# An S4D + dense + LoRA tower on one core: the first two x1 tiles turned by TensorE in fp32, four W2 squares and the bias pass moved

## The reference

```python
# tok: the S4D kernel, L = 1024 steps
dt  = exp(log_dt);  A = -exp(inv_A_real) + 1j*A_imag;  dtA = A*dt[:, None]
Cc  = B[None]*x_complex * (exp(dtA) - 1) / A
h   = 2 * real(einsum('chn,hnl->chl', Cc, exp(dtA[:, :, None]*arange(1024))))
# attn: layernorm without gain, then a dense 1024 x 1024 product
h   = h + (layernorm(h) @ attn_W.T + attn_b)
# ffn: layernorm, dense product, and a mixture of 4 LoRA experts of rank 8
z   = layernorm(h)
h   = h + (z @ W.T + b) + sum_e softmax(z @ Wr.T)_e * 2 * ((z @ A_e.T) @ Bm_e.T)
```

## Time and profile before

| what | value |
|---|---|
| time, median of 3 runs | 831.0 us (828.77 to 832.25) |
| the profiled execution's own time | 829.42 us |
| its span | 827.6 us |
| mean granted clock of TensorE | 0.987 of full |
| TensorE busy | 792.3 us, 96% |
| VectorE busy | 583.2 us, 70% |
| ScalarE busy | 394.8 us, 48% |
| DMA moved | 70.17 MB |

### The profile page before, as it was taken

How to read it: one execution, slowest core, us unless ns; L and a number is a source line. 1 busy time by engine, 2 the same in 40 slices (tenths; PEclk the granted TensorE clock), 3 DMA queues, 4 the chain that set the end, 5 groups by cost and what they waited for, 6 DMA issues and landing times.

```text
span 827.6 us, 15856 instructions
## 1 busy us (share of the span) xinstructions
PE 792.3 (96%) x5974; PEld 410.0 (50%) x5974; DVE 583.2 (70%) x1136; ACT 394.8 (48%) x778; POOL 7.1 (1%) x20
## 2 busy tenths in 40 slices
PE   3678899999999999999999999999999999999998
PEld 3653445554554455455545554555455545554543
DVE  7889786766757777776768777676877767676533
ACT  4658643626454462636355272645436264642210
POOL 2000000000000000000000000000000000000000
PEclk9889999999999999999999999999999999999999
DMA  7637633424332232334232333433324243323323
GB/s 273 192 72 160 121 77 71 92 54 95 76 79 67 64 82 65 81 76 93 62 80 57 76 78 67 95 76 63 70 64 95 52 94 76 89 51 76 53 51 76
DMA packets 185563, 70.17 MB, mean 85 GB/s; under 512 B 174080, under 2 KB 179072, under 8 KB 185544
## 3 DMA queue, kind: packets, MB, share of 16 engines
q1 hardware_dynamic: 185448, 69.80, 36.9%
q10 hardware_dynamic: 96, 0.13, 0.0%
HBM read 11.96 MB, written 16.78 MB: 35 GB/s over the span
## 4 chain that ended last, share of the span: by engine, by line
PE 89%; DVE 7%; ACT 2%; issue 1%; DMA 0%; SPq 0%; DVEq 0%; ACTq 0%
PE ps_g L523 38%; PE ps_g L463 38%; PE ps_a L455 7%; PE ps_g L534 2%; PE ps_g L651 1%; PE ps_p L511 1%; DVE wa_lo L1181 1%; DVE params L932 1%; DVE m_im L1042 1%; PE ps_p L513 1%; DVE h_tok L1051 0%; DVE m L1042 0%; PE ps_p L528 0%; ACT phase L690 0%; DVE y L1076 0%
## 5 line engine op out<-in xcount | busy, mean ns | idle before, releaser
L463 PE MATMUL ps_g<-wa_hi,x 128*128 128x512 f16 x1024 | 271.5, 381 | 2.9 <-DMA x<-x_tok 2.2
L523 PE MATMUL ps_g<-wf_hi,x 128*128 128x512 f16 x992 | 265.2, 380 | 1.7 <-DVE h_tok L1090 1.7
L463 PEld LDWEIGHTS ps_g<-wa_hi,x 128*128 128x128 f16 x1024 | 97.9, 98 | 123.2 <-issue 7.4
L463 PE MATMUL ps_g<-wa_lo,x 128*128 128x512 f16 x512 | 154.0, 380 | 0.0
L523 PE MATMUL ps_g<-wf_lo,x 128*128 128x512 f16 x496 | 149.2, 380 | 0.0
L523 PEld LDWEIGHTS ps_g<-wf_hi,x 128*128 128x128 f16 x992 | 95.0, 98 | 107.8 <-issue 2.5
L716 ACT ACTIVATE junk<-ps_a,stat 128x1024 bf16<-128x1024 f32 x32 | 35.7, 1114 | 121.8 <-DVE stat L1054 121.8
L736 ACT ACTIVATE x_tok<-y 128x1024 f16<-128x1024 f32 x32 | 33.8, 1057 | 125.3 <-DVE y L1076 125.3
L1152 DVE SCALAR_TENSOR_TENSOR result<-ps_g,unscale,h_tok 128x1024 f32<-128x1024 f32 x31 | 39.8, 1284 | 72.1 <-PE ps_g L534 72.1
L463 PEld LDWEIGHTS ps_g<-wa_lo,x 128*128 128x128 f16 x512 | 50.3, 98 | 60.6 <-issue 1.0
L722 ACT ACTIVATE junk<-h_tok,stat 128x1024 bf16<-128x1024 f32 x32 | 36.7, 1147 | 91.1 <-DVE stat L1094 91.1
(11 more groups left out here) (188 smaller groups left out, 759.5 us busy)
## 6 DMA issues: line engine op xcount, KB each, us to landing
out<-result SPq DMA_DIRECT2D x124, 128.0 KB, 2.2
stage<-in_L_ffn_W SPq DMA_DIRECT2D x8, 512.0 KB, 8.5
x_raw<-in_x SPq DMA_DIRECT2D x38, 64.0 KB
h_tok<-in_L_attn_weight SPq DMA_DIRECT2D x2, 512.0 KB, 4.1
x<-in_L_attn_weight SPq DMA_DIRECT2D x2, 512.0 KB, 7.6
result<-in_L_attn_weight SPq DMA_DIRECT2D x2, 512.0 KB, 9.2
x<-x_tok SPq DMA_TRANSPOSE x64, 3.2
x<-stage SPq DMA_TRANSPOSE x64, 2.8
```

What stands on the lines that cost most here:

```text
L463: mm = pe.matmul(ps[:, o, :], x1_part(part, ps is ps_g2)[:, k, :], ws[:, k, o * HALF:(o + 1) * HALF], start=k == 0 and part == 0 and ws is ...
L523: pe.matmul(ps_g2[:, o, :], xs[:, k, :], ws[:, k, o * HALF:(o + 1) * HALF], start=k == 0 and xs is x2_hi and ws is wf_hi, stop=False)
```

## The change

- x1 of the sub-tiles (0, 0) and (0, 1) is no longer split to `x1_tok` and turned by DMA. TensorE turns `y` in fp32, in two halves of four transposes, into `ps_x` and `ps_p` (`turn_first_x1`). ScalarE copies each half to the high part of x1 (`high_first`), VectorE subtracts it from PSUM for the low part (`low_first`). The counts of `s_x1`, `s_hi1`, `s_lo1` are two sub-tiles lower from then on (`X1_BY_PE`).
- In TensorE's order the squares of the W2 blocks 8 to 11 stand ahead of the q transposes. Before, 8 and 9 stood behind `turn_weight(0)`, and 10 and 11 behind `s4(0, 0)`.
- The second pass over the bias on ScalarE moves from behind `first_decays(1)` to ahead of the copies of q, and the small op on VectorE that it needs to the front of its order.
- `weight_norms(1)` moves ahead of `normalise_1(0, 0)` and writes its product to a free part of `params`.
- The orders of `ffn_hi`/`ffn_lo` for blocks 8 and 9, of `attn_hi`/`attn_lo` and of `make_m(0, 1)` shift around these; `SPLITS` and `LOWS` follow.

```diff
-SPLITS = (0, 1, 2, 3, 4, 5, 8, 6, 9, 7, 10, 11, 12, 13, 14, 15)
-LOWS = (0, 1, 2, 3, 4, 5, 8, 6, 7, 9, 10, 11, 12, 13, 14, 15)
+SPLITS = (0, 1, 2, 3, 4, 5, 6, 8, 7, 9, 10, 11, 12, 13, 14, 15)
+LOWS = (0, 1, 2, 3, 4, 5, 6, 7, 8, 9, 10, 11, 12, 13, 14, 15)
+X1_BY_PE = 2
...
@@ sync
             sp.wait_ge(s_norm, 2)
-            turn_x1(0, 0)
             load_x(1)
             turn_weights(KB, KB + 1)
             sp.wait_ge(s_wt, KB)
             load_lora_a(wg_rows, s_wg)
-            turn_x1(0, 1)
             turn_weights(KB + 1, KB + 5)
@@ tensor
+            def turn_first_x1(i):
+                pe.wait_ge(s_xn1, i + 1)
+                for half, ps in enumerate((ps_x, ps_p)):
+                    for k in range(4):
+                        block = 4 * half + k
+                        mm = pe.transpose(ps[:, k * P:(k + 1) * P], y[:, block * P:(block + 1) * P], ident[:, :])
+                    mm.then_inc(s_yt, 1)
...
             turn_x(0)
+            pe.wait_ge(s_pre_act, 3)
+            square_ffn(KB, KB + 4)
             pe.wait_ge(s_pre_act, 6)
...
             turn_weight(0)
-            pe.wait_ge(s_xt_sb, 1)
-            pe.wait_ge(s_pre_act, 3)
-            square_ffn(KB, KB + 2)
             pe.wait_ge(s_top, 1)
             turn_weight(1)
             pe.wait_ge(s_q, 2)
             s4(0, 0)
-            square_ffn(KB + 2, 2 * KB)
+            square_ffn(KB + 4, 2 * KB)
             square_lora_a()
...
             turn_weight(3)
+            pe.wait_ge(s_xt_sb, 1)
+            pe.wait_ge(s_top, 2)
+            turn_first_x1(0)
             pe.wait_ge(s_wlo, low_done(3))
             turn_weight(4)
-            pe.wait_ge(s_top, 2)
+            pe.wait_ge(s_lo1_half, 2)
             turn_weight(5)
+            attn_part(0, 0, range(0, 4), (0,))
             pe.wait_ge(s_wlo, low_done(4))
             turn_weight(6)
-            pe.wait_ge(s_x1, 32)
-            attn_part(0, 0, range(0, 4), (0,))
             s4(0, 1)
...
-            attn_part(0, 0, range(KB), (1,)).then_inc(s_g1, 1)
+            attn_part(0, 0, range(0, 5), (1,))
+            turn_first_x1(1)
+            attn_part(0, 0, range(5, KB), (1,)).then_inc(s_g1, 1)
+            pe.wait_ge(s_lo1_half, 4)
             turn_x(1)
             turn_lora_a()
-            pe.wait_ge(s_x1, 64)
             attn_part(0, 1, range(0, 6), ps=ps_g2)
@@ scalar
+            def high_first(i):
+                for half, ps in enumerate((ps_x, ps_p)):
+                    act.wait_ge(s_yt, 2 * i + half + 1)
+                    act.activation(x1_part(0, i == 1)[:, 4 * half:4 * half + 4, :],
+                                       ps[:, :].rearrange("p (k o) -> p k o", o=P), ACT.Copy).then_inc(s_hi1_half, 1)
...
-            high_1(0, 0)
-            attn_hi(2, 3)
-            attn_hi(4, 5)
+            attn_hi(2)
+            high_first(0)
+            attn_hi(3, 4, 5)
+            attn_hi(6)
             ffn_hi(8)
-            attn_hi(6)
-            ffn_hi(9)
             attn_hi(7)
             square_1(0, 1)
             rstd_guess(0, 1, stat_1, s_ssq1, s_log1, s_y1)
+            ffn_hi(9)
+            high_first(1)
             ffn_hi(10)
-            high_1(0, 1)
@@ vector
+            def low_first(i):
+                for half, ps in enumerate((ps_x, ps_p)):
+                    part = slice(4 * half, 4 * half + 4)
+                    dve.wait_ge(s_hi1_half, 2 * i + half + 1)
+                    dve.tensor_tensor(x1_part(1, i == 1)[:, part, :], ps[:, :].rearrange("p (k o) -> p k o", o=P),
+                                      x1_part(0, i == 1)[:, part, :], ALU.subtract).then_inc(s_lo1_half, 1)
...
             keep_h(0, 0)
             attn_lo(0, 1)
+            weight_norms(1, ps_p[:, 0:P])
             normalise_1(0, 0)
-            low_1(0, 0)
-            attn_lo(2, 3)
-            dve.wait_ge(s_lo1, 1)
-            weight_norms(1, ps_p[:, 0:P])
+            attn_lo(2)
+            low_first(0)
+            attn_lo(3)
             make_first_u(1)
             split_scales(1)
-            attn_lo(4)
             make_m(0, 1)
-            attn_lo(5)
-            ffn_lo(8)
+            attn_lo(4, 5)
             attn_lo(6)
             keep_h(0, 1)
             attn_lo(7)
             normalise_1(0, 1)
+            ffn_lo(8)
+            low_first(1)
             ffn_lo(9)
-            low_1(0, 1)
             ffn_lo(10, 11, 12)
```

More of the change, by code:

```diff
@@ L206, in program @@
         s_x1, s_x2 = sem("x1_transposed"), sem("x2_transposed")
+        s_yt = sem("first_normalised_halves_transposed")
+        s_hi1_half, s_lo1_half = sem("first_x1_hi_halves_ready"), sem("first_x1_lo_halves_ready")
         s_g1 = sem("attn_product_done")
@@ L352, in turn_x1 @@
             def turn_x1(t, i):
[L354 to L362, removed]
+                sp.wait_ge(s_g1, 2 * t + i)
+                sp.wait_ge(s_hi1, 2 * t + i + 1 - X1_BY_PE)
+                sp.dma_start_transpose(x1_part(0), by_token(x1_tok[:, :], 0)).then_inc(s_x1, 16)
+                sp.wait_ge(s_lo1, 2 * t + i + 1 - X1_BY_PE)
+                sp.dma_start_transpose(x1_part(1), by_token(x1_tok[:, :], 1)).then_inc(s_x1, 16)
             def turn_x2(t, i):
@@ L397, in _ @@
                          allow_slow_non_contiguous=True).then_inc(s_lb, 16)
-            sp.wait_ge(s_norm, 2)
-            turn_x1(0, 0)
             load_x(1)
@@ L468, in attn @@
             def attn(t, i):
-                pe.wait_ge(s_x1, 32 * (2 * t + i + 1))
+                pe.wait_ge(s_x1, 32 * (2 * t + i + 1 - X1_BY_PE))
                 at_least(pe, s_h2, 2 * t + i)
@@ L734, in high_1 @@
                 act.wait_ge(s_xn1, 2 * T + i + 1)
-                at_least(act, s_x1, 32 * (2 * T + i))
+                if not isinstance(T, int) or 2 * T + i > X1_BY_PE:
+                    act.wait_ge(s_x1, 32 * (2 * T + i - X1_BY_PE))
                 act.activation(by_token(x1_tok[:, :], 0), y[:, :], ACT.Copy).then_inc(s_hi1, 1)
+            def high_first(i):
[3 more added lines that the diff above has]
+                                       ps[:, :].rearrange("p (k o) -> p k o", o=P), ACT.Copy).then_inc(s_hi1_half, 1)
             def high_2(t, i):
@@ L793, in _ @@
                 .then_inc(s_bias_act, 1)
+            act.wait_ge(s_bias_dve, 1)
+            act.activation(bias_bc[:, :], bias_bc[:, :], ACT.Identity, bias=bias_stat[:, 1:2],
+                           accum_out=bias_stat[:, 2:3]).then_inc(s_bias_act, 1)
             act.wait_ge(s_pre_pe, 3)
@@ L799, in _ @@
             first_decays(1)
-            act.wait_ge(s_bias_dve, 1)
-            act.activation(bias_bc[:, :], bias_bc[:, :], ACT.Identity, bias=bias_stat[:, 1:2],
-                           accum_out=bias_stat[:, 2:3]).then_inc(s_bias_act, 1)
             attn_hi(0, 1)
@@ L1074, in normalise_1 @@
                 newton(J, stat_1, s_y1, s_nw1)
-                at_least(dve, s_lo1, J)
+                at_least(dve, s_lo1, J - X1_BY_PE)
                 dve.tensor_scalar(y[:, :], whole(ps_a), stat_1[:, 1:2], stat_1[:, 7:8],
@@ L1079, in low_1 @@
             def low_1(T, i):
-                dve.wait_ge(s_hi1, 2 * T + i + 1)
-                at_least(dve, s_x1, 32 * (2 * T + i))
+                dve.wait_ge(s_hi1, 2 * T + i + 1 - X1_BY_PE)
+                if not isinstance(T, int) or 2 * T + i > X1_BY_PE:
+                    dve.wait_ge(s_x1, 32 * (2 * T + i - X1_BY_PE))
                 dve.tensor_tensor(by_token(x1_tok[:, :], 1), y[:, :], by_token(x1_tok[:, :], 0), ALU.subtract)\
                     .then_inc(s_lo1, 1)
+            def low_first(i):
[4 more added lines that the diff above has]
+                                      x1_part(0, i == 1)[:, part, :], ALU.subtract).then_inc(s_lo1_half, 1)
             def keep_h2(t, i, ps=ps_g1):
@@ L1157, in weight_norms @@
                 dve.wait_ge(s_norm, k + 1)
-                dve.scalar_tensor_tensor(out=y[:, k * P:(k + 1) * P], in0=ps, scalar=1.0, in1=ident[:, :],
+                at_least(dve, s_top, k)
+                dve.scalar_tensor_tensor(out=params[:, 1140:1140 + P], in0=ps, scalar=1.0, in1=ident[:, :],
                                          op0=ALU.mult, op1=ALU.mult, accum_out=top[:, k, 0:1]).then_inc(s_top, 1)
@@ L1213, in split_lora_b @@
                                   ALU.subtract).then_inc(s_lbn, 1)
+            dve.wait_ge(s_bias_act, 1)
+            dve.tensor_scalar(bias_stat[:, 1:2], bias_stat[:, 0:1], -1 / L, None, ALU.mult).then_inc(s_bias_dve, 1)
             round_turns(0)
@@ L1220, in _ @@
             make_first_u(0)
-            dve.wait_ge(s_bias_act, 1)
-            dve.tensor_scalar(bias_stat[:, 1:2], bias_stat[:, 0:1], -1 / L, None, ALU.mult).then_inc(s_bias_dve, 1)
             split_scales(0)
```

## The result

| | before | changed |
|---|---|---|
| median of 20 runs each | 830.29 us (828.56 to 832.25) | 833.70 us (831.04 to 835.79) |
| ratio, 95% interval | | 1.0040 (1.0029 to 1.0050) |
| the profiled execution's own time | 829.42 us | 831.68 us |
| its span | 827.6 us | 829.9 us |
| mean granted clock | 0.987 | 0.988 |

The change costs 3.4 us, 0.4%. It was forecast as +3.4 us, but part of that agreement is luck: the profiled execution is only 2.3 us longer than that of before. What the median adds to it comes, as far as the runs show, from TensorE's clock, which I had priced at zero. The absolute forecast of 834.4 us also stood on a time of before that was 0.7 us too high (831.0 of three runs against 830.29 of twenty).

A forecast was written before the change was run, and what follows sets the result against it. VectorE's written order, not TensorE, was taken to set the loop's entry. Stall 3.2 + bias 0 + x1 0.2 + clock 0 = +3.4 us on 831.0 gave 834.4 us, range 830 to 837.5.

The forecast's parts named there:

- Entry, not pace: Main loop: TensorE is busy throughout, so the change only shifts loop entry; an entry x us later ends x us later.
- Part 1, the squares: Before the q transposes: squares wait for W2 block 11, landing at 25.8 us, so the transposes start 3.2 us later.
- Part 2, the bias: ScalarE's bias pass moves into its 3.29 us wait for the q transposes: price 0, at most 0.1 us.
- Part 3, x1: keep_h(0, 0) to keep_h2(0, 1): VectorE's stream 0.2 us longer, ends -0.6 to +1.0; TensorE freed, VectorE not.
- the two waits on VectorE: In the x1 stretch: VectorE waits 1.1 us for turn_weight(6) and 1.0 us for the copied first half of x1.
- One sign: Wait before the FFN product, 1.70 us in the kernel before, was claimed to become longer.
- Part 4, the clock: Loop entry to the end of s4(1, 0): 0 taken, leaning to a loss; 2.2 us worse to 1.7 better possible.
- The sum: Whole kernel: 3.2 stall + 0 bias + 0.2 x1 + 0 clock = +3.4 us.
- Rival 2, the colder clock: First FFN matmuls and all of s4(1, 0) run at 1.2 GHz after longer idling: 836.6 us, chance 0.20.
- The bounds of the forecast: Whole kernel, without the rivals: 832.7 to 835.7 us, including 0.5 us each way.
- rival 3: Loop entry: TensorE's lead, products 3.3 us sooner, reaches it with squares in the gap: 827.7 us, chance 0.10.
- Rival 4: After the fp32 transposes the clock stays low, so s4(0, 0) adds 1.9 us: 836.3 us, chance 0.03.

The follow-up runs named there:

- before with the squares early: Kernel before with only the squares of W2 blocks 8 to 11 moved ahead of the q transposes: 832.43 us, ratio 1.0027 to before.
- squares back: Changed kernel with only the squares of W2 blocks 8 to 11 put back where they stood before: 831.52 us, ratio 1.0014 to before.
- both are filled: Unread matmuls around project(0, 0), 8 + 6 in the kernel before and 22 + 5 in squares back: 827.73 and 827.75 us.
- the filled pair: Changed kernel and squares back, each with 22 + 5 unread matmuls around project(0, 0): 830.82 and 827.75 us, ratios 1.0013 and 0.9973 to before.
- the three low-clock profiles: Changed kernel with squares of two W2 blocks early, before with blocks 8 to 11 early, changed kernel with six early: medians 830.20, 832.43, 837.13 us.

## Why the prediction was right, point by point

- **Entry, not pace.** Right. From 120 to 620 us TensorE is busy all the time in both profiles, and `s4(1, 1)` moved by 104.34 - 102.08 = 2.26 us against 2.3 us of span.
- **Part 1, the squares.** The mechanism is right, the size was off: 2.5 us of delay in the profiled execution where I had 3.2. The squares of block 11 took the 0.83 us that I gave them (24.76 to 25.59). The landing was early: `sync` issued the W2 loads from 15.17 us on and not from 16.14. Over the fourteen profiles of this case they start between 14.54 and 16.14, and the 16.14 that I had read is the latest. The delay itself varies with it: 3.2 us in before with the squares early.
- **Part 2, the bias.** Right: it ran at 23.80 in ScalarE's gap, and `keep_h(0, 0)` waited for `s4` alone.
- **Part 3, x1.** Right to 0.1 us in its sum: VectorE's stream is 0.2 us longer. The place is luck: `ffn_lo(10)` comes 30.5 us behind `keep_h(0, 0)` against 30.4 before, and most of the 0.2 lies behind it (a wait for ScalarE of 0.46 us instead of 0.28). `low_first` took 0.69 (0.7 taken), the copies 0.60 (0.69), the two waits on VectorE 0.85 and 1.08 (1.0 and 1.1), the wait for the LoRA rows 1.33 (1.3). In squares back TensorE had its products at 76.9 (77 taken). Of the 3.7 us by which that is earlier than the 80.6 of before, 1.7 are the lower clock behind the x1 wait in before's profile, which I had not read and which not every execution has. One sign was put wrongly: I said that the wait before the FFN product would exceed 1.70 us. That one fell to 1.45, and it is the wait before `project` that grew, to 5.58.
- **Part 4, the clock.** This term failed: "I take 0". The profiled stretch indeed costs the same (0.70 both times), but over many runs the clock costs about 1 us more: squares back is 1.1 us above before (0.1 to 2.2), 1.7 us in the group with the lower clock and 0.5 in the other, and not above it once both are filled. The 1.1 us is only just clear of noise. The place was only half right as well: beside the stretch before `s4(1, 0)` it is `s4(1, 1)`, behind its wait of 2.1 us.
- **The sum** of +3.4 is therefore 2.2 us of stall (3.1 by the filled pair) and the rest, 0.3 to 1.2 us, clock, not 3.2 and 0. That the two add up to the forecast is luck. Rival 2, the colder clock, is true in part, in half of the runs. But TensorE was not at 1.2 GHz for all of the stretch, which took 6.1 to 6.4 us in the three low-clock profiles and not 7.8; most of the loss lay at `s4(1, 1)`. The low-clock group at 834.5 us lies below the 836.6 of that rival. The bounds of the forecast hold 0.5 us each way for which no row is given, and rival 3 counts 3.3 us where part 3 has 80.6 - 77 = 3.6.
- **Rival 4.** In the changed kernel's profile TensorE did transposes alone from 25.59 to 30.90 us. The granted clock was 0.50 up to 28.9 and 1.00 from 29.0 on, and `s4(0, 0)` ran at full clock, 1.95 us, after a wait of 2.54 us. By the rule that would bring the rival about, transposes do not count as activity for the clock (the Trainium skill, TensorE: Matmul & The Clock Gate, Part 4: PE-mode transpose). Neither this trace nor the earlier trace rows agrees with it. Two other executions with early squares have `s4(0, 0)` at 2.48 and 2.80 us, 0.5 and 0.8 more, not 1.9. Why those and not the changed kernel's is not shown. No run here has transposes and nothing else for longer than these 5.3 us.

## What to carry to other kernels

An idle gap is free for new work only if the work's own inputs are there: work put into it brings its waits along, and in an in-order queue they fall on whatever stands behind. When an engine is relieved, look for the engine whose written order releases the next stage; here one instruction that stood behind three others on VectorE started some 3.5 us later than it could have. And a lead that is not used turns into idle time, after which TensorE's clock was lower for the next work, in some runs and not in others. So compare many runs and their clocks, and not one profile.

## What had not been expected of the hardware

- The times of one kernel go with its granted clock in groups, 1.6 us apart for before and 2.8 us for the changed kernel. After waits of 2.1 to 2.4 us TensorE's clock was full in some executions and between 0.54 and 0.76 in others, at the same place of the program. Filling the idle time before the FFN with unread matmuls took the changed kernel with the squares back from 831.52 to 827.75 us (1.0014 to 0.9973 of before).
- Issue times of DMAs differ between executions: the eight W2 loads begin between 14.54 and 16.14 us in fourteen profiles of kernels whose order there is the same. A margin of 1.5 us against one of these loads, read from one profile, is not safe.
